# A small attention block with routed experts: u turned in float32, scores 2 in three products of 64 rows side by side, and the tail's expert pairs in another order

## What is computed

```python
# block 1, over channels-first x: [4, 64, 1024]
q, k, v = wq @ x, wk @ x, wv @ x                 # 32 channels each
att = softmax(einsum('bmi,bmj->bij', k, q), 2)   # 1024 x 1024 for each image
x = x + wo @ einsum('bij,bmj->bmi', att, v)
t = tokens(x)                                    # [4, 1024, 64]
# block 2
u = layernorm(t)
t = t + softmax(u @ u.T) @ u                     # "scores 2" is u @ u.T
# block 3
w = layernorm(t)
p = softmax(w @ router_w + router_b)             # 8 experts, the best 2 kept, renormalized
t = t + sum_over_2_best(p_e * (w @ expert_w[e] + expert_b[e]))
out = channels_first(t)
```

## Time and profile before

| | us | share of the span |
|---|---|---|
| median of 3 runs | 217.2 | |
| profiled execution | 217.16 | |
| its span | 215.4 | |
| PE busy | 201.7 | 94% |
| PEld busy | 103.6 | 48% |
| DVE busy | 144.9 | 67% |
| ACT busy | 107.2 | 50% |
| POOL busy | 61.5 | 29% |

### The profile page before, as it was taken

How to read it: one execution, slowest core, us unless ns; L and a number is a source line. 1 busy time by engine, 2 the same in 40 slices (tenths; PEclk the granted TensorE clock), 3 DMA queues, 4 the chain that set the end, 5 groups by cost and what they waited for, 6 DMA issues and landing times.

```text
span 215.4 us, 2921 instructions
## 1 busy us (share of the span) xinstructions
PE 201.7 (94%) x1067; PEld 103.6 (48%) x1067; DVE 144.9 (67%) x359; ACT 107.2 (50%) x164; POOL 61.5 (29%) x75
## 2 busy tenths in 40 slices
PE   7999899899999899998999999899999999898993
PEld 2646443455534345543443554354353334386772
DVE  3899867889348882594688745628694262898970
ACT  3623775377644564574356446566453765301110
POOL 8140041202000300012003469600378840026250
PEclk9999999999999999999999999999999999999999
DMA  3852000000000000000000000100000002000021
GB/s 108 149 147 50 3 0 0 0 2 3 2 0 0 0 3 0 0 0 0 3 2 0 0 3 2 38 11 3 0 0 0 0 3 50 0 0 3 0 49 49
DMA packets 3501, 3.67 MB, mean 17 GB/s; under 512 B 2208, under 2 KB 2464, under 8 KB 3488
## 3 DMA queue, kind: packets, MB, share of 16 engines
q1 hardware_dynamic: 3248, 3.45, 6.9%
q10 hardware_dynamic: 240, 0.05, 0.1%
HBM read 2.45 MB, written 1.05 MB: 16 GB/s over the span
## 4 chain that ended last, share of the span: by engine, by line
PE 69%; DVE 20%; ACT 4%; POOL 3%; issue 2%; DVEq 0%; POOLq 0%
PE acc L494 21%; DVE rowmax L1121 7%; PE ring L555 6%; PE ring L600 6%; PE ring L556 5%; PE ring L487 5%; PE ring L469 5%; PE acc L630 3%; POOL sm L370 3%; PE acc L636 2%; PE ring L445 2%; PE ring L531 2%; PE ring L542 2%; DVE stats L1154 2%; PE ring L458 1%
## 5 line engine op out<-in xcount | busy, mean ns | idle before, releaser
L908 ACT ACTIVATE prob<-ring,shift 128x1024 f32<-128x1024 f32 x32 | 35.5, 1111 | 27.6 <-PE ring L556 27.5
L1121 DVE TENSOR_REDUCE rowmax<-ring 128x1 f32<-128x1024 f32 x32 | 38.1, 1217 | 12.8 <-PE ring L469 12.6
L370 POOL TENSOR_TENSOR sm<-sm,minus_half 128x8 f32<-128x8 f32 x8 | 15.8, 1974 | 101.9 <-DVE sm L1164 101.9
L905 ACT ACTIVATE prob<-ring 128x1024 f32<-128x1024 f32 x32 | 32.0, 1023 | 18.2 <-PE ring L487 18.1
L494 PE MATMUL acc<-prob,u 128*64 128x512 f32 x128 | 31.0, 606 | 0.0
L494 PE MATMUL acc<-prob,val 128*64 128x512 f32 x128 | 31.0, 605 | 0.0
L1260 DVE TENSOR_TENSOR prod<-ring,gate 128x1024 f32<-128x1024 f32 x16 | 19.4, 1220 | 9.3 <-PE ring L600 8.8
L555 PE MATMUL ring<-zst 128*128 128x512 f16 x64 | 24.6, 384 | 0.4 <-DVE rowmax L1121 0.4
L556 PE MATMUL ring<-zsw,zst 128*128 128x512 f16 x64 | 24.3, 379 | 0.0
L469 PE MATMUL ring<-qst,kst 96*128 96x512 f32 x64 | 22.0, 433 | 0.7 <-DVE rowmax L1121 0.4
L487 PE MATMUL ring<-kst,qst 98*128 98x512 f32 x64 | 21.5, 425 | 1.1 <-DVE kst L1118 0.5
(11 more groups left out here) (156 smaller groups left out, 308.6 us busy)
## 6 DMA issues: line engine op xcount, KB each, us to landing
xin<-in_x SPq DMA_DIRECT2D x6, 256.0 KB, 4.0
out<-ob SPq DMA_DIRECT2D x6, 128.0 KB, 2.3
xin<-in_x SPq DMA_DIRECT2D x4, 128.0 KB, 2.9
e_in<-in_L_ffn_expert_w SPq DMA_DIRECT2D x2, 128.0 KB
out<-ob SPq DMA_DIRECT2D x4, 64.0 KB, 2.0
eb_in<-in_L_ffn_expert_b SPq DMA_DIRECT2D x8, 2.0 KB
wo<-in_L_conv_wo SPq DMA_DIRECT2D x2, 8.0 KB, 2.3
r_in<-in_L_ffn_router_w SPq DMA_DIRECT2D x2, 2.0 KB
```

The lines of the kernel that those rows point to most:

```text
L370: pool.tensor_tensor(sm[:, 3, :], sm[:, 2, :], minus_half[:, :], ALU.pow).then_inc(s_rs, 1)
L905: act.activation(prob1[:, j % DEEP, :], flat(filled(act, f"st{j}", b)), ACT.Exp).then_inc(s_p1, 1)
L908: act.activation(prob2[:, j % DEEP, :], flat(filled(act, f"s{j}", b)), ACT.Exp, bias=shift[:, :], accum_out=rsum2[b % 2][:, j:j + 1]).then ...
L1121: dve.tensor_reduce(rowmax[:, tile:tile + 1], flat(filled(dve, f"mx{tile}", b)), AX.X, ALU.max).then_inc(s_mx, 1)
```

## The change

u is turned as it is: 16 float32 matmuls of `u` (64 columns held) against the identity, each tile once into rows 0 to 63 and once into rows 64 to 127 of one ring buffer. The split comes behind the turn. ACT rounds it to `z_hi`, DVE subtracts `z_hi` for `z_lo`, both 128 x 1024, and then the buffer is free. The fp16 copies and `ident_h` go. A group of scores 2 is now three products, high x high, high x low, low x high, each in two halves of 64 rows, as the experts have them. `route` does all products with `w_hi` first and waits for `w_lo` after them. In the tail, experts 3,2 stand ahead of image 2's last additions, the turned gates of image 3 between these, experts 3,3 ahead of the sums of image 3, and ACT copies the gates before the result of image 2.

```diff
...
@@ -262,7 +258,7 @@
         def release(name, b):
 
             table = {"w3": (s_wts, 3), "q": (s_qs, b + 2), "k": (s_ks, b + 2), "vx": (s_vx, 2 * b + 2),
-                     "mr": (s_mrow, 2 * b + 2), "po": (s_po, b + 1), "uT": (s_z, 2 * b + 2),
+                     "mr": (s_mrow, 2 * b + 2), "po": (s_po, b + 1), "uT": (s_z, b + 1),
                      "wT": (s_ws, b + 1), "rt": (s_lg, b + 1), "yT": (s_ob, b + 1)}
             if name in table:
                 return table[name]
@@ -534,26 +530,26 @@
 
             def u_transposed(b):
                 buf = take("uT", b)
-                pe.wait_ge(s_uh, b + 1)
-                pe.wait_ge(s_u, b + 1)
-                for which in (1, 0):
-                    for tile in range(T):
-                        c = col(tile)
-                        mm = pe.transpose(buf[:, which, :].bitcast(F16)[:, c:c + P],
-                                          uhl[:, tile, which:which + 2, :].rearrange("p a c -> p (a c)"), ident_h[:, :])
-                    if which:
-                        mm.then_inc(s_uT, 1)
+                pe.wait_ge(s_un, b + 1)
+                for tile in range(T):
+                    c = col(tile)
+                    for h in range(2):
+                        mm = pe.matmul(flat(buf)[h * C:(h + 1) * C, c:c + P], u[b % 2][:, tile, :], ident[:, :],
+                                       start=True, stop=True)
                 mm.then_inc(s_fill, 1)
 
             def scores2(b, j):
                 buf = take(f"s{j}", b)
                 if j == 0:
-                    pe.wait_ge(s_z, 2 * (b + 1))
-                straight, swapped = zst[b % 2], zsw[b % 2]
-                z = straight[:, col(j):col(j) + P]
-                for h in range(2):
-                    pe.matmul(buf[:, h, :], z, straight[:, h * CHUNK:(h + 1) * CHUNK], start=True, stop=False)
-                    mm = pe.matmul(buf[:, h, :], z, swapped[:, h * CHUNK:(h + 1) * CHUNK], start=False, stop=True)
+                    pe.wait_ge(s_z, b + 1)
+
+
+                high, low = z_hi[b % 2], z_lo[b % 2]
+                for n, (held, moving) in enumerate(((high, high), (high, low), (low, high))):
+                    for h in range(2):
+                        rows = slice(h * C, (h + 1) * C)
+                        mm = pe.matmul(buf[:, h, :], held[rows, col(j):col(j) + P],
+                                       moving[rows, h * CHUNK:(h + 1) * CHUNK], start=(n == 0), stop=(n == 2))
                 mm.then_inc(s_fill, 1)
 
             def y_transposed(b):
@@ -580,14 +576,16 @@
 
             def route(b):
                 buf = take("rt", b)
-                pe.wait_ge(s_ws, b + 1)
+                pe.wait_ge(s_wr, b + 1)
                 if b == 0:
                     pe.wait_ge(s_es, 4)
-                for g in range(T // 2):
-                    where = buf[:, 0, g * 4 * E:(g + 1) * 4 * E]
-                    both = r_blk[:, :, :, :].rearrange("p h a e -> p (h a e)")
-                    pe.matmul(where, w_hi[b % 2][:, g * P:(g + 1) * P], both, start=True, stop=False)
-                    mm = pe.matmul(where, w_lo[b % 2][:, g * P:(g + 1) * P], both, start=False, stop=True)
+                both = r_blk[:, :, :, :].rearrange("p h a e -> p (h a e)")
+                for part in (w_hi, w_lo):
+                    if part is w_lo:
+                        pe.wait_ge(s_ws, b + 1)
+                    for g in range(T // 2):
+                        mm = pe.matmul(buf[:, 0, g * 4 * E:(g + 1) * 4 * E], part[b % 2][:, g * P:(g + 1) * P], both,
+                                       start=(part is w_hi and g == 0), stop=(part is w_lo and g == T // 2 - 1))
                 mm.then_inc(s_fill, 1)
 
             def experts(b, g):
@@ -854,16 +852,17 @@
             route(3)
             experts(3, 0)
             experts(3, 1)
+            experts(3, 2)
             for t in range(1, 4):
                 pe.wait_ge(s_half, (T // 2) * 2 + t)
                 add_experts(2, t, E // 2, acc1[:, t * P:(t + 1) * P], t == 3)
-            experts(3, 2)
-            gates_transposed(3)
+                if t == 2:
+                    gates_transposed(3)
+            experts(3, 3)
             pe.wait_ge(s_ob, 3)
             pe.wait_ge(s_tk2, B)
             pe.wait_ge(s_gt, B)
             start_sums(3, range(2), acc1)
-            experts(3, 3)
             for t in range(2):
                 pe.wait_ge(s_half, (T // 2) * 2 + 4 + t)
                 add_experts(3, t, E // 2, acc1[:, t * P:(t + 1) * P], t == 1)
@@ -916,14 +915,8 @@
                 act.wait_ge(s_av2, b + 1)
                 act.activation(att2[:, :], sum2[b][:, :], ACT.Copy).then_inc(s_att2, 1)
 
-            def copy_high(b):
-                act.wait_ge(s_un, b + 1)
-                act.activation(uhl[:, :, 2, :], u[b % 2][:, :, :], ACT.Copy).then_inc(s_uh, 1)
-
-            def stack_swapped(b):
-                buf, _ = PLACE[("uT", b)]
-                act.wait_ge(s_uT, b + 1)
-                act.activation(zsw[b % 2][:, :], ring[:, buf, 1, :].bitcast(F16), ACT.Copy).then_inc(s_z, 1)
+            def round_z(b):
+                act.activation(z_hi[b % 2][:, :], flat(filled(act, "uT", b)), ACT.Copy).then_inc(s_zr, 1)
 
             def round_w(b):
                 act.activation(w_hi[b % 2][:, :], filled(act, "wT", b)[:, 0, :], ACT.Copy).then_inc(s_wr, 1)
@@ -1002,10 +995,9 @@
             exp1(1, 3)
             round_k(2)
             exp1(1, 4)
-            copy_high(0)
             values(2)
             exp1(1, 5)
-            stack_swapped(0)
+            round_z(0)
             exp1(1, 6)
             exp1(1, 7)
 
...
@@ -1089,10 +1078,10 @@
             copy_gates(2)
             round_w(3)
             gap_exp(3)
+            copy_gates(3)
             act.wait_ge(s_out[0], 32)
             act.wait_ge(s_sums, 4)
             act.activation(ob[0][:, :], acc1[:, :], ACT.Copy).then_inc(s_ob, 1)
-            copy_gates(3)
             b = B - 1
             act.wait_ge(s_out[b % 2], 32)
             act.wait_ge(s_sums, 6)
@@ -1176,14 +1165,12 @@
                 dve.wait_ge(s_cen1, b + 1)
                 dve.wait_ge(s_rs1, b + 1)
                 dve.tensor_tensor(own[:, :, :], cen1[:, :, :], wide(sm1[:, 3, :], C), ALU.mult).then_inc(s_un, 1)
-                dve.wait_ge(s_un, b + 1)
-                dve.tensor_copy(uhl[:, :, 0, :], own[:, :, :]).then_inc(s_uh1, 1)
-                dve.wait_ge(s_uh1, b + 1)
-                dve.tensor_tensor(uhl[:, :, 1, :], own[:, :, :], uhl[:, :, 0, :], ALU.subtract).then_inc(s_u, 1)
-
-            def stack_u(b):
-                buf = filled(dve, "uT", b)
-                dve.tensor_copy(zst[b % 2][:, :], buf[:, 0, :].bitcast(F16)).then_inc(s_z, 1)
+
+            def split_z(b):
+                buf, _ = PLACE[("uT", b)]
+                dve.wait_ge(s_zr, b + 1)
+                dve.tensor_tensor(z_lo[b % 2][:, :], flat(ring[:, buf]), z_hi[b % 2][:, :].bitcast(F32),
+                                  ALU.subtract).then_inc(s_z, 1)
 
             def tokens2(b):
 
@@ -1308,11 +1295,9 @@
                 rows = slice(h * C, (h + 1) * C)
                 dve.tensor_tensor(r_blk[rows, h, 1, :], r_in[rows, :], r_blk[rows, h, 0, :].bitcast(F32),
                                   ALU.subtract).then_inc(s_es, 1)
-            dve.tensor_copy(ident_h[:, :], ident[:, :])
             row_max(1, 6)
             row_max(1, 7)
             negate_max(1)
-            dve.tensor_copy(ident_h[:, :], ident[:, :])
             max_row(1)
 
             tokens1(0)
...
```

More of the change, by code:

```diff
@@ L131, in build @@
         u = two("u", [P, T, C])
-        zst = two("zst", [P, N], F16)
-        zsw = two("zsw", [P, N], F16)
+        z_hi = two("z_hi", [P, N], F32R)
+        z_lo = two("z_lo", [P, N], F32R)
         rsum2 = two("rsum2", [P, T])
@@ L150, in build @@
         cen1 = sb("cen1", [P, T, C])
-        uhl = sb("uhl", [P, T, 3, C], F16)
         rinv2 = sb("rinv2", [P, T])
@@ L222, in build @@
         s_un = sem("u_step")
-        s_uh1 = sem("u_high_ready")
-        s_uh = sem("u_high_copied")
-        s_u = sem("uhl_ready")
-        s_uT = sem("u_transposed")
-        s_z = sem("z_ready")
+        s_zr = sem("z_rounded")
+        s_z = sem("z_split")
         s_p2 = sem("probs2_ready")
@@ L1019, in _ @@
             exp2(0, 4)
-            copy_high(1)
             exp2(0, 5)
-            stack_swapped(1)
+            round_z(1)
             exp2(0, 6)
@@ L1044, in _ @@
             exp2(1, 4)
-            copy_high(2)
             exp2(1, 5)
-            stack_swapped(2)
+            round_z(2)
             exp2(1, 6)
@@ L1071, in _ @@
             exp2(2, 4)
-            copy_high(3)
             exp2(2, 5)
-            stack_swapped(3)
+            round_z(3)
             exp2(2, 6)
@@ L1339, in _ @@
             row_max(2, 6)
-            stack_u(1)
+            split_z(1)
             row_max(2, 7)
@@ L1361, in _ @@
             weigh_experts(0, 0)
-            stack_u(2)
+            split_z(2)
```

(2 more changed lines are left out.)

3 lines of the change are left out of this document (1 added, 2 removed).

## The result

The changed kernel takes 219.28 us, the median of seven runs (219.27 to 219.92), against 217.2 before: a ratio of 1.0092, with a 95% interval of 1.0074 to 1.011. Its profiled execution took 219.27, with a span of 217.5. So the change costs 2.1 us where +2.75 was forecast. The prediction drew the line of what can be told from no change at 219.4: the median lies just under it, where 22 of the forecast's own 62 in 100 lay, while the side above it had been given 57.

What follows compares the result with a forecast made beforehand. TensorE, busy 94% of a 215.4 us span, bounds the kernel by its order of work. Terms -0.6 + 4.3 + 0.7 - 0.55 - 0.1 - 1.0 = +2.75 on 217.16 give 219.9 us, range 217.8 to 222.2.

Steps and rivals of the forecast that it cites:

- The turn, +4.3: Four turns of u on TensorE: 1.93 us each with entry and exit, plus 0.15 for image 0's new borders, +4.3 us.
- run side by side: The turn's two column halves overlap, 1.8 us; the rival that they don't, 3.6 each, gave 227.1 us, 7%.
- The issue-bound rival: Rival at the turn of u: instruction issue limits it to about 2.0 us, 220.7 us in all, 10%.
- Scores 2, -0.6: 32 groups of scores 2: three pairs for four products save 5.3 us, nearly all paid back at borders, -0.6 us.
- The stall behind the turn of image 2, +0.7: TensorE waits for the turn's ring buffer, held until ACT has rounded and DVE subtracted, +0.7 us.
- So I count nothing: y's chain slides 1.65 where TensorE slid 1.3; the wait for w of image 1 eats the extra 0.35.
- What waits absorb, -0.55: Existing TensorE waits take up 0.2 at q and 0.2 at row maxima of image 3, 0.15 at image 2's projection.
- ident_h, -0.1: The identity's fp16 copy vanishes from DVE's path to the last row maxima of image 1, -0.1 us.
- The tail, -1.0: Route starting on w_hi and the reordered end let the last additions start at 209.4 instead of 210.34, -1.0 us.
- DVE's relief: Rival: stalls in front of y and for q of image 3 close up instead of moving along, 218.3 us, 9%.
- No turn ran at 0.9: Rival at the four turns: each takes 0.9 in place of 1.8 us, so 216.3 us, not slower, 7%.
- The changes of division are not free: Rival: switching TensorE between 128-row and 64-row work costs nothing where three products follow, instead of 0.19 each; 215.2 us, 5%.

Runs made afterwards that it cites:

- experiment 3: The changed kernel, but DVE writes u twice side by side and TensorE turns it in eight float32 128x128 transposes: 215.65 us, ratio 0.9926.
- experiment 1: The kernel before with only the new route and tail: 216.09 us; the reverse, the changed kernel with the old route and tail: 220.55 us.
- experiment 2: The changed kernel with each turn's 16 matmuls reordered, eight into rows 0 to 63, then eight into rows 64 to 127: 225.05 us in one run.
- the last kernel: The second kernel of experiment 8, but GpSimd begins image 0's residual only when DVE has written wn of image 1: 214.09 us, ratio 0.9851.
- experiment 6: The changed kernel with scores2(1,6) and the weighing pair ahead of image 0's second expert group: 221.53 us, ratio 1.0195.
- experiment 8: Experiment 3 with w's root first on GpSimd and y turned after image 3's last scores 1: 216.78 us; second kernel adds experiment 6's order: 215.15 us.
- experiments 7: y of image 0 turned two score groups later, right ahead of w's turn, on experiment 6's kernel: 221.29 us; same order on experiment 3: 217.29 us.

## Why the prediction was right, point by point

The forecast, slower by about 2.7 for the turn, held in its mechanism: experiment 3 takes away the turn's form alone and gets 3.6 back, and experiment 1 shows what the tail gives.

The same places before and after, by their starts on TensorE, show where the time came in:

| place | before | after | later by |
|---|---|---|---|
| turn of image 0 | 55.16 | 55.06 | -0.10 |
| turn of image 1 | 78.83 | 79.60 | 0.77 |
| turn of image 2 | 119.93 | 121.49 | 1.56 |
| scores2(1,6) | 122.56 | 125.84 | 3.28 |
| turn of y of image 0 | 136.59 | 140.05 | 3.46 |
| turn of w of image 1 | 140.36 | 143.56 | 3.20 |
| turn of image 3 | 160.01 | 162.70 | 2.69 |
| experts 3,0, ahead of route | 195.71 | 198.91 | 3.20 |
| the last additions | 210.34 | 212.48 | 2.14 |

- **The turn, +4.3.** Measured 1.90 each, against 0.86 to 0.88 and, for image 3, 0.99 before: +4.0. Ahead of image 0's turn the new border is 0.08, where 0.15 was put. The form was right and its step a little too dear, 0.109 where 0.112 was put; the 0.15 for entry and exit is what 16 such steps leave of 1.90. That they run side by side was right (experiment 2). The issue-bound rival asked for 2.0 a turn, 0.1 more than measured. Against it speaks that a step with two records takes as long as a step with one (experiment 2).
- **Scores 2, -0.6.** The prices hold. The pairs stand 0.23 apart. A group takes 0.79 behind experts (from the row below to the turn at 121.49) and 0.89 with a change on both sides (152.65 to 153.54, further down).

```profile
120.70 0.40 PE L551 MATMUL ring<-z_hi 64*128 64x512 f32 x2
```

  Between two groups of whole-array work the neighbours grow too. The projection, one group of scores 2 and the turned gates, before and after:

```profile
148.35 1.11 PE L531 MATMUL ring<-wo_blk,agg 128*128 128x130 f32 x8
...
150.36 1.94 PE L494 MATMUL acc<-prob,u 128*64 128x512 f32 x8
```

```profile
151.56 1.16 PE L527 MATMUL ring<-wo_blk,agg 128*128 128x130 f32 x8
152.65 0.50 PE L551 MATMUL ring<-z_hi 64*128 64x512 f32 x2
...
153.81 1.94 PE L490 MATMUL acc<-prob,u 128*64 128x512 f32 x8
```

  2.01 became 2.25, +0.24, where -0.165 and two borders of 0.19 make +0.215. Yet the total is the term that was mis-sized. Take from the 3.20 ahead of the tail the turns (4.0), the stall (0.75), the waits (-0.65, below), the identity's copy (-0.15) and y's and w's part (+0.1): about -0.85 is left for scores 2 with their borders and the turn's, where the forecast had -0.6 and +0.15, so -0.45. That is a remainder, and which of the 64 borders it lies at was not sorted out. Much of it came in among experts: between 152.24 and the turn of image 3 at 160.01 in the kernel before, the lag falls from 3.43 to 2.69.
- **The stall behind the turn of image 2, +0.7.** 0.60 idle, 0.75 by starts, at the predicted place and with the predicted releaser.
- **"So I count nothing" for y and w.** Right in its course as well: y's turn slides by 0.36 more than what stands ahead of it (the forecast's extra 0.35), and the wait for w behind it then eats 0.25. The reason was thinner than I knew: w doesn't hang on TensorE's work alone but on which of GpSimd's additions meets which of DVE's steps. In the kernel after, one DVE step of 128x8 at 138.69 takes 1.25 beside y's addition; in the kernel before, its addition for tok at 133.63 took 1.67. One collision was exchanged for another of about the same size, which the prediction had no means to count on: that part was luck.
- **What waits absorb, -0.55.** By the waits of TensorE, grouped by line and releaser (us in all, times, the longest), before and after:

```profile
PE ring L478 <- DVE nmax L1129: 1.4, 2, 1.0
PE ring L445 <- DVE qst L1113: 1.0, 1, 1.0
...
PE ring L531 <- ACT agg L913: 0.4, 1, 0.4
...
PE ring L555 <- DVE rowmax L1121: 0.4, 1, 0.4
```

```profile
PE ring L474 <- DVE nmax L1118: 1.2, 2, 0.9
...
PE ring L441 <- DVE qst L1102: 0.8, 1, 0.8
...
PE ring L551 <- DVE rowmax L1110: 0.3, 1, 0.3
...
PE ring L527 <- ACT agg L912: 0.2, 1, 0.2
```

  The waits for q and for the projection shrank as counted (0.21 and 0.15 in the timelines). So did the second row maximum group of image 3, from 1.46 (86.49 to 87.95) to 1.29:

```profile
88.49 1.35 PE L465 MATMUL ring<-qst,kst 96*128 96x512 f32 x4
```

  The weighing behind it starts at 89.78. That makes 0.53. Only the wait in front of the first scores 2 (0.12) was not on my list. The smaller wait for the negated row maxima is the next term, not one of these.
- **ident_h, -0.1.** The longer of the two waits for the negated row maxima, that of image 1, went from 1.04 to 0.91, and TensorE goes on at 42.15 instead of 42.31.
- **The tail, -1.0.** -1.06 in the trace; 1.1 and about 1.1 by experiments 1 and 2.
- **The other rivals.** DVE's relief didn't close the stall in front of y, which grew to 1.16, and the one for q only by the 0.2 counted. No turn ran at 0.9. The changes of division are not free: 0.10 between 0.79 and 0.89, and +0.24 for the group between whole-array work.

So forecast and measurement differ by 0.6: about 0.4 at scores 2 and the borders, 0.1 to 0.2 at the turns, 0.1 at a wait that wasn't listed, and less than 0.1 at each of the rest, with 0.1 for y and w against it.

Not settled: why the clock falls in some executions of a kernel and not in others. And the last kernel stacks three edits on experiment 3's; how much of its 1.56 under that kernel is the order of experiment 6 wasn't tried apart. In its trace 1.06 of it is there when the attention of image 1 is turned (131.49 instead of 132.55), ahead of what GpSimd's new order touches.

## What to carry to other kernels

Count borders before counting products: a cheaper form with other rows in use pays on each side, and three pairs for four whole products came out nearly even. Count the records of a float32 turn before choosing its form: eight transposes took 0.85 us with u written twice, where 16 products on column halves took 1.90. Before you move work on the busiest engine, follow the chains of the others to where it next waits for them: here three kernels that removed a stall of 0.6 to 0.9 by reordering got one of 2.4 to 2.6, and what helped was to keep two helper engines from running at the same moment. And look at the clock of each execution before reading a median: in experiment 8 one median lay between two kinds of them, where no execution was.

## What the runs showed of the hardware

- Two float32 records on 64 columns each, 128 columns moved, take 0.109 us a step, side by side, as one record alone does (0.110); the turn's 32 records take 1.90 us with the halves as neighbours and 3.26 with the same halves one after the other.
- A group of three pairs takes 0.79 us behind 64-row work and 0.89 behind 128-row work, and put between two groups of 128-row work in place of four whole products it makes the three together 0.24 longer, though it saves 0.165 itself.
- A DVE step on 128x8 went from 0.17 to 1.25 us, and one on 128x512 from 0.69 to 1.79, beside a GpSimd addition on 128x512.
- TensorE's granted clock fell behind waits of 2.57, 2.35, 2.36, 1.76 and 1.68 us in the profiled executions (to 0.53 to 0.59 over the 3.1 to 3.6 us that follow, in the four read), and not behind waits of 1.16 and 0.65. The executions of the kernels of experiments 7 and 8 come with a mean granted clock of 1.0 or of 0.984 to 0.992, and the latter are 1.2 to 2.9 us longer.
- The kernel before has such executions too: beside the experiments 8 of its 55 took 218.21 to 219.27 at 0.984 to 0.991, the others 217.04 to 217.54 at 0.997 or more. No profile of one of the eight exists, so where the clock fell in them isn't shown; TensorE's longest waits past its first in the profiled one are 1.04 and 1.01.
